# Attention scores of a two-layer block: from bf16 products over 96 rows, one head at a time, to float32r products of two heads in the two row halves of TensorE

## The chip, the cores and the metric

The kernel runs on one core of one Trainium2 chip. The metric is the device time of one execution in microseconds (us), lower is better; it is the median over several executions. The kernel is written straight against the engines: each engine has its own list of instructions, and semaphores order them against each other.

## What is computed

Two transformer layers on a tensor `x` of 2 batches x 512 tokens x 512 features, all in float32. Each layer normalises `x`, and adds an attention branch and a gated feed-forward branch that both read the normalised `x`:

```python
xn = _layernorm(x, axis=-1)
x = x + _L0_attn_ref(xn, ...) + _L0_ffn_ref(xn, ...)
xn = _layernorm(x, axis=-1)
x = x + _L1_attn_ref(xn, ...) + _L1_ffn_ref(xn, ...)
# attention of both layers, H = 32 heads of HD = 16 features, T = 512 tokens
scores = einsum('bhqd,bhkd->bhqk', q, k)            # causal, scaled by 1/sqrt(HD)
weights = softmax(scores, axis=-1)
ctx = einsum('bhqk,bhkd->bhqd', weights, v)         # then @ Wo + bo
# layer 0 shares the keys and values of 8 groups among 32 heads
# feed-forward: down(silu(gate(x)) * up(x)), 1792 hidden features, then 1376
```

## The kernel before

**The dense work.** Every dense product is made of three float32r products: both operands are split into a high part, rounded to float32r, and a low part (`three_passes`, L1245). The weights come in chunks of 128x512 (256 KB) over the SP queue; ACT makes the high part `w_hi` (L988), POOL the low part `w_lo` (L921). A projection step (`proj`) takes one chunk and issues 12 matmuls of 128x512 into a bank of `g_ring` (2 banks); the steps `out` and `v1` issue matmuls of 128x256 into the two `acc` banks, `v0` those of 128x128.

**Attention** is cut into 32 units: 4 phases (layer, batch) x 8 units of four heads each (`4 * QUADS`). A unit has 10 jobs; a job fills one PSUM bank of 512 columns with causal blocks. All four heads of a unit have four query tiles of 128; a tile attends to 128, 256, 384 or 512 keys. For a unit there are these steps:

- `S` (L1358), 10 per unit: the scores with queries as rows. A head has only 16 features; both operands are split into three bf16 parts each, and `Q_PARTS` and `K_PARTS` stack six products of parts, so the contraction is 6 x 16 = 96 rows. DVE adds the causal mask and takes each row's maximum (`smax`, L1213).
- `msplit` on POOL (L943 to L947) splits the negated maxima into three bf16 parts, `Mt` (L1366) transposes them, `mrow` (L1223) copies them out, and two DMAs put them as rows 96 to 98 under the queries of `q_op`; under the keys of `k_op` stand rows of ones.
- `T` (L1381), 10 per unit: the scores again, with keys as rows and 96 + 3 = 99 contraction rows, so that the maximum is already subtracted. ACT takes the exponential of the bank's 512 columns (`exp`, L981), POOL masks the diagonal blocks (`mask`, L968).
- `PV` (L1399), 3 per unit: the masked exponentials times the values and a column of ones, in full float32, four heads side by side in column tiles of 17 (heads at partitions 0, 32, 64, 96 of `pv_ps`). ACT copies the result (`oev`, L994), `otr` (L1408) transposes it, DVE divides by the sums (`norm`).

`S`, `T` and `Mt` share a ring of three PSUM banks (`s_ring`, `wait_ring`). The queries and keys of eight heads (an octet) go from `proj` through `qhi` (ACT, L1030), `qres` (DVE, L1154), `qmid` (ACT, L1035) and `qlo` (POOL, L933) to DRAM and come back with six DMAs each (L866), one per stacked part.

**The order of the work** on each engine is made by `plan()`: a list `fill` of dense steps in fixed order, and queues of attention steps with a due place in it (`S_AT`, `T_AT`, `PV_AT`). It goes by tables of costs (`PE_US`, `ACT_US`, ...). Nearly every attention step thus stands between dense steps.

**The start** has 22 matmuls that only keep PE at work (L1268), then the layer norms of both batches. Of these early tiles the first is normalised on DVE (L1123) and eleven on POOL (L928); each is transposed by PE (L1281) into `g_ring`, from which ACT and DVE make `xt_hi` and `xt_lo`.

## Time and profile before

| what | value |
|---|---|
| median of 3 executions | 942.08 us (941.6 to 943.6) |
| the profiled execution, its time | 943.2 us |
| its span in the profile | 941.6 us |
| PE busy | 887.2 us (94%) |
| DVE, ACT, POOL busy | 524.5, 458.0, 497.5 us |
| DMA | 91.01 MB, mean 97 GB/s |
| mean granted TensorE clock | 0.98 |

PE is TensorE's matmul side, PEld its weight loads, SP the queue that issues all DMAs. Matmuls are pipelined: a row's duration runs from the issue of a matmul to its modelled end and overlaps the next ones. What a matmul costs when the engine is full is therefore the distance between the starts of two following rows, not the duration in them. In a timeline the first number is the start in us, the second the duration in us, and what stands in brackets is the idle time before it and what ended it.

### The profile page before, as it was taken

What the parts mean: (1) busy time and instruction counts of PE and PEld (TensorE: products, weight loads), DVE (VectorE), ACT (ScalarE), POOL (GpSimd) and SP (SyncE); (2) the same over time, 40 slices, a digit from 0 to 9 for tenths busy, and PEclk for the clock granted to TensorE, in tenths of its full rate; (3) what the DMA queues carried; (4) which work ended last, traced back from release to release, by engine and by line L of the source; (5) the groups of instructions that cost most, each with busy time, mean ns of one, the idle gap of its engine ahead of it and who ended that gap; (6) DMA issues with size and microseconds to landing.
All of it is one profiled execution on the core that took longest, in us unless ns stands there. A gap on an engine that the chain in (4) does not pass through costs nothing. (4 is left out here: it accounts for less than half of the span.)

```text
span 941.6 us, 16765 instructions
## 1 busy us (share of the span) xinstructions
PE 887.2 (94%) x5790; PEld 645.2 (69%) x5790; DVE 524.5 (56%) x1543; ACT 458.0 (49%) x838; POOL 497.5 (53%) x747
## 2 busy tenths in 40 slices
PE   6778999999999899999999999999999999999887
PEld 3654655666788666677678886677667876566677
DVE  5455454756756656644576566545476474454353
ACT  2343444545646435444475555444375454344542
POOL 6834445453565534555555665455455666454343
PEclk7889999999999999999999999999999999999999
DMA  6534151523241421527172642827344463721131
GB/s 190 123 106 105 41 119 36 119 68 87 77 89 58 108 68 47 119 84 154 57 145 71 148 95 75 159 67 136 90 113 106 107 140 106 149 63 61 54 90 35
DMA packets 62146, 91.01 MB, mean 97 GB/s; under 512 B 9104, under 2 KB 31120, under 8 KB 62064
## 3 DMA queue, kind: packets, MB, share of 16 engines
q1 hardware_dynamic: 62064, 89.95, 39.6%
q8 instruction: 47, 0.77, 0.3%
q14 instruction: 35, 0.29, 0.1%
HBM read 77.21 MB, written 12.71 MB: 95 GB/s over the span
## 5 line engine op out<-in xcount | busy, mean ns | idle before, releaser
L921 POOL TENSOR_TENSOR w_lo<-w_raw,w_hi 128x512 fp32r<-128x512 f32 x204 | 268.3, 1320 | 84.6 <-ACT w_hi L988 80.8
L981 ACT ACTIVATE p<-s_ring 128x512 f32<-128x512 f32 x320 | 183.4, 597 | 175.2 <-PE s_ring L1381 174.5
L1213 DVE CUSTOM_DVE_ANT_0 s_ring<-s_ring,causal 128x384 f32<-128x384 f32 (+3 forms) x512 | 239.0, 515 | 48.1 <-PE s_ring L1358 47.2
L968 POOL TENSOR_SCALAR_AFFINE_SELECT p<-p 128x256 f32<-128x256 f32 (+1 forms) x320 | 121.0, 381 | 255.2 <-ACT p L981 252.8
L1245 PE MATMUL g_ring<-xt_hi,w_hi 128*128 128x512 f32 (+1 forms) x504 | 214.4, 425 | 6.8 <-DVE xt_lo L1143 3.1
L1245 PE MATMUL g_ring<-xt_lo,w_hi 128*128 128x512 f32 (+1 forms) x504 | 200.2, 397 | 0.0
L1245 PE MATMUL g_ring<-xt_hi,w_lo 128*128 128x512 f32 (+1 forms) x504 | 199.6, 396 | 0.0
L988 ACT ACTIVATE w_hi<-w_raw 128x512 fp32r<-128x512 f32 x204 | 127.6, 627 | 51.0 <-PE acc L1245 25.0
L1381 PE MATMUL s_ring<-q_op,k_op 99*128 99x384 bf16 (+3 forms) x512 | 118.8, 304 | 12.3 <-DVE maxima L1213 6.2
L1245 PE MATMUL acc<-w_hi,h_hi 128*128 128x256 f32 (+1 forms) x400 | 123.3, 308 | 4.1 <-DVE h_lo L1194 4.1
L1358 PE MATMUL s_ring<-k_op,q_op 96*128 96x384 bf16 (+3 forms) x512 | 115.8, 303 | 8.9 <-DVE maxima L1213 4.5
L1245 PEld LDWEIGHTS g_ring<-xt_hi,w_hi 128*128 128x128 f32 (+1 forms) x504 | 96.4, 191 | 35.4 <-DVE xt_lo L1140 3.8
L1245 PE MATMUL acc<-w_lo,h_hi 128*128 128x256 f32 (+1 forms) x400 | 113.7, 284 | 0.0
L1245 PE MATMUL acc<-w_hi,h_lo 128*128 128x256 f32 (+1 forms) x400 | 113.3, 283 | 0.0
L1194 DVE TENSOR_TENSOR h_lo<-h,h_hi 128x512 fp32r<-128x512 f32 (+1 forms) x100 | 90.6, 918 | 38.0 <-ACT h_hi L1041 37.8
L1245 PEld LDWEIGHTS g_ring<-xt_hi,w_lo 128*128 128x128 f32 (+1 forms) x504 | 96.2, 191 | 22.2
L1245 PEld LDWEIGHTS g_ring<-xt_lo,w_hi 128*128 128x128 f32 (+1 forms) x504 | 96.6, 192 | 17.4
L1399 PE MATMUL pv_ps<-p,v_op 128*17 128x512 f32 (+3 forms) x1024 | 88.5, 440 | 0.2 <-POOL p L968 0.2
L1245 PEld LDWEIGHTS acc<-w_hi,h_hi 128*128 128x128 f32 (+1 forms) x400 | 76.8, 192 | 10.3 <-issue 7.4
L1179 DVE SCALAR_TENSOR_TENSOR gate<-gate,g_ring 128x512 f32<-128x512 f32 (+1 forms) x50 | 34.4, 688 | 87.2 <-ACT gate L1000 87.2
L1358 PEld LDWEIGHTS s_ring<-k_op,q_op 96*128 96x128 bf16 x512 | 39.0, 98 | 64.1 <-ACT p L981 21.8
L1381 PEld LDWEIGHTS s_ring<-q_op,k_op 99*128 99x128 bf16 x512 | 37.6, 98 | 63.5 <-DVE maxima L1213 23.0
(86 smaller groups left out, 1138.9 us busy)
## 6 DMA issues: line engine op xcount, KB each, us to landing
w_raw<-weights_in SPq DMA_DIRECT2D x204, 256.0 KB, 2.7
q_op<-qk_scratch SPq DMA_DIRECT2D x96, 128.0 KB, 4.4
qk_scratch<-qk_parts SPq DMA_DIRECT2D x26, 384.0 KB, 2.6
k_op<-qk_scratch SPq DMA_DIRECT2D x48, 128.0 KB, 4.3
x<-x_in SPq DMA_DIRECT2D x8, 256.0 KB, 4.5
y_out<-x SPq DMA_DIRECT2D x8, 256.0 KB, 2.6
k_op<-qk_scratch SPq DMA_DIRECT2D x24, 64.0 KB, 3.0
bo_all<-bo_in SPq DMA_DIRECT2D x2, 256.0 KB, 5.1
```

Of the source, the lines that this page charges most:

```text
L921: pool.tensor_tensor(w_lo[:, c % SPLIT, :], w_raw[:, c % RAW, :], w_hi[:, c % SPLIT, :].bitcast(F32), ALU.subtract).then_inc(split_done, 1)
L968: pool.affine_select(out=view, in_=view, compare_op=ALU.is_ge, fill=0.0, base=0, pattern=[[0, n], [1, P]] if n == 2 else [[1, P]], channel ...
L981: act.activation(p32[:, j % PRING, :], s_ring[r % SRING][:, :], ACT.Exp, scale=SCALE).then_inc(exp_done, 1)
L988: act.activation(w_hi[:, c % SPLIT, :], w_raw[:, c % RAW, :], ACT.Copy).then_inc(whi_done, 1)
L1179: dve.scalar_tensor_tensor(out=gate[0:m, n % 2, :], in0=gate[0:m, n % 2, :], scalar=1.0, in1=g_ring[g % 2][0:m, :], op0=ALU.add, op1=ALU.m ...
L1194: dve.tensor_tensor(h_lo[0:rows, hs % HSPLIT, :], h[0:rows, f, :], h_hi[0:rows, hs % HSPLIT, :].bitcast(F32), ALU.subtract).then_inc(hlo_d ...
L1213: last = dve.tensor_tensor_reduce(out=s_ring[r % SRING][:, at:at + n], in0=s_ring[r % SRING][:, at:at + n], in1=causal[:, 512 - n:], scale ...
L1245: ins = pe.matmul(dst, w[a], xa[c], start=first and i == 0, stop=last and i == 2, skip_group_check=skip)
L1358: last = pe.matmul(s_ring[r % SRING][:, at:at + n], q_op[0:QROWS, u // 2 % 2, 4 * (u % 2) + j, qt * P:(qt + 1) * P], k_op[0:QROWS, ks, kh, ...
L1381: last = pe.matmul(s_ring[r % SRING][:, at:at + n], k_op[0:MROWS, ks, kh, kt * P:(kt + 1) * P], q_op[0:MROWS, u // 2 % 2, 4 * (u % 2) + j, ...
L1399: last = pe.matmul(pv_ps[32 * j:32 * j + VW, kt * P:T], v_op[:, slot, kt, vh, :], p32[:, (JOBS * u + job) % PRING, at:at + T - kt * P], st ...
```

## The change

- The operands of the scores are no longer bf16 but float32r, in high and low parts: a query stands as (high, low, high), a key as (high, high, low), so a product has 3 x 16 = 48 rows, and `T` has 50, since the maximum is now two rows. The steps `qmid`, `qlo` and `msplit` are gone; `Mt` transposes the float32 maxima, and `mrow` makes both parts in two DVE instructions.
- Even heads stand on partitions 0 to 49, odd heads on 64 to 113 of `q_op` and `k_op` (`ROW_TILE = 64`, `operands`). Two jobs, one of an even and one of an odd head, are issued block by block in turn, each into its own bank.
- A PE step `ST` (a visit) issues two jobs of `S` and two of `T`, the latter 7 visits behind. There are 5 visits per unit, 167 in all (the first 7 have only `S`, the last 7 only `T`). `S` has two banks `s_bank`, `T` two in one tensor `t_banks`. Before it a visit waits for the maxima of the visit before, and ahead of its `T` part for the exponential of the visit before.
- ACT takes one exponential of 128x1024 over both `t_banks` (L1004), 160 in place of 320.
- `PV` is one step of all 16 products per unit instead of three, and takes a bank of `g_ring`; `pv_ps` is gone.
- The queries and keys go to DRAM already stacked (three DMAs of 256 KB) and come back with two DMAs of 48 partitions; layer 0's keys are read again for every octet (`kin`).
- At the start all early tiles are normalised on DVE, four at a time, and transposed into the four score banks; 28 and 8 matmuls keep PE at work in place of 22, and the second octet's queries are projected in the start.
- The planner's constants and the places of the steps are set anew.

```diff
-MROWS = QROWS + 3
-Q_PARTS = (0, 0, 1, 0, 1, 2)
-K_PARTS = (0, 1, 0, 2, 1, 0)
+QROWS = 3 * HD
...
+def score_blocks(job):
+
+    if job < 4:
+        return ((job, 3, 0),)
+    if job < 8:
+        return ((job - 4, 0, 3 * P), (job - 4, 2, 0))
+    return ((job - 8, 1, 0), (job - 6, 1, 2 * P))
+
+
...
+RAW, SPLIT, HSPLIT, PRING, EARLY_BANKS = 4, 4, 3, 14, 4
+VISITS = JOBS // 2
+LAG = VISITS + 2
+SCORE_VISITS = 4 * QUADS * VISITS
...
+        def begin():
+            if kind == "x":
+                ln_stats(0, b)
+            else:
+                ln_rms(b)
+            for tt in range(TT):
+                end["xn", first + tt] = place("dve", at("stats", 0, b, kind), "xn", 0, b, kind, tt,
+                                              ("early", first + tt), first + tt)
...
+    def filler(i, count):
+        return [(0.0, lambda: 0.0, lambda: line["pe"].append((state["t"], len(line["pe"]), ("busy", i, count))))]
+
+    q1 = w_octet(0, 1, 0)
+    prologue = (ln_0 + filler(0, 8) + ln_1[:1] + q + k0 + ln_1[1:3] + w_v(0, 0, 0) + ln_1[3:] + k1 + w_v(0, 1, 1) + ln_n[:3] + q1
+                + ln_n[3:] + rms_1)
     ffn00 = w_ffn(0, 1)
...
-        q_op = sb("q_op", [MROWS, 2, 8, T], BF16)
-        k_op = sb("k_op", [MROWS, 2, 8, T], BF16)
+        q_op = sb("q_op", [P, 2, 4, T], F32R)
+        k_op = sb("k_op", [P, 2, 4, T], F32R)
...
-        s_ring = [ctx.enter_context(nc.psum_tensor(f"s_ring{i}", [P, 512], F32)) for i in range(SRING)]
+        s_bank = [ctx.enter_context(nc.psum_tensor(f"s_bank{i}", [P, 512], F32)) for i in range(2)]
+        t_banks = ctx.enter_context(nc.psum_tensor("t_banks", [P, 2, 512], F32))
+        t_bank = [t_banks[:, i, :] for i in range(2)]
...
+        def operands(u, j):
+
+            rows = ROW_TILE * (j % 2)
+            slot, pair = u // 2 % 2, 2 * (u % 2) + j // 2
+            k_pair = u % 2 if u < 2 * QUADS else pair
+            return rows, slot, pair, k_pair
...
                 elif kind == "qkin":
                     _, n, what, l, b, octet = s
...
+                    dst, here = (q_op, q_here) if what == "q" else (k_op, k_here)
+                    if octet >= 2:
+                        sp.wait_ge(t_made, t_count(2 * octet - 3))
+                    for half in range(2):
+                        rows = ROW_TILE * half
+                        sp.dma_start(dst[rows:rows + QROWS, octet % 2, :, :].bitcast(F32),
+                                     qk_scratch[n % 2].rearrange("r (p two) t -> two r p t", two=2)[half]
+                                     ).then_inc(here[octet % 2], 16)
...
-                elif kind == "xn":
...
-                    pool.tensor_scalar(h[:, own, :], x[:, b * TT + tt, :], mv[:, b, tt, 0:1],
-                                       scale[:, b, tt:tt + 1], ALU.subtract, ALU.mult).then_inc(xn_pool_done, 1)
-                elif kind == "qlo":
...
-                elif kind == "msplit":
...
                 if kind == "exp":
-                    _, r, j, i = s
-                    act.wait_ge(ring_made, n_ring[r])
+                    _, j, u, i = s
+                    act.wait_ge(t_made, t_count(u, i))
                     if j >= PRING:
-                        act.wait_ge(pv_done, n_pv[pv_of_job(j - PRING)])
-                    act.activation(p32[:, j % PRING, :], s_ring[r % SRING][:, :], ACT.Exp, scale=SCALE
+                        act.wait_ge(pv_done, 4 * n_pv[(j + 1 - PRING) // JOBS])
+                    act.activation(p32[:, j % PRING:j % PRING + 2, :], t_banks[:, :, :], ACT.Exp, scale=SCALE
                                    ).then_inc(exp_done, 1)
...
                 elif kind == "smax":
-                    _, r, u, i = s
-                    dve.wait_ge(ring_made, n_ring[r])
-                    if i == 0 and u == 0:
+                    _, u, job = s
...
+                    bank = s_bank[job % 2]
+                    for j, qt, at in score_blocks(job):
                         n = (qt + 1) * P
+                        column = 8 * (j % 2) + 4 * (j // 2) + qt
...
-                elif kind == "S":
-                    _, r, u, i = s
-                    wait_ring(r)
...
-                    for j, qt, at in score_blocks(i):
-                        n = (qt + 1) * P
-                        ks, kh = k_slot_and_head(u, j)
-                        last = pe.matmul(s_ring[r % SRING][:, at:at + n],
-                                         q_op[0:QROWS, u // 2 % 2, 4 * (u % 2) + j, qt * P:(qt + 1) * P],
-                                         k_op[0:QROWS, ks, kh, 0:n], start=True, stop=True)
-                    last.then_inc(ring_made, 1)
+                elif kind == "ST":
+                    v = s[1]
+                    if v < SCORE_VISITS:
+                        u, i = divmod(v, VISITS)
+                        if i:
+                            pe.wait_ge(smax_done, max(n_smax[(u, 2 * i - 2)], n_smax[(u, 2 * i - 1)]))
+                        elif u:
+                            pe.wait_ge(smax_done, n_smax[(u - 1,)])
+                        else:
+                            pe.wait_ge(g_freed, max(last_early[0], last_early[1]))
+                        if i == 0:
+                            octet = u // 2
+                            pe.wait_ge(q_here[octet % 2], arrival[("q", octet)])
+                            pe.wait_ge(k_here[octet % 2], arrival[("k", octet)])
+                        blocks = [score_blocks(job) for job in (2 * i, 2 * i + 1)]
+                        for n_block, pair in enumerate(zip(*blocks)):
+                            for j, qt, at in pair:
+                                n = (qt + 1) * P
+                                r, slot, p, kp = operands(u, j)
+                                ins = pe.matmul(s_bank[j % 2][:, at:at + n],
+                                                q_op[r:r + QROWS, slot, p, qt * P:(qt + 1) * P],
+                                                k_op[r:r + QROWS, slot, kp, 0:n], start=True, stop=True)
+                                if n_block == len(blocks[0]) - 1:
+                                    ins.then_inc(s_made, 1)
+                    if v >= LAG:
+                        t_u, i = divmod(v - LAG, VISITS)
+                        if v > LAG:
+                            pe.wait_ge(exp_done, n_exp[JOBS * t_u + 2 * i - 2])
+                        else:
+                            pe.wait_ge(g_freed, max(last_early[2], last_early[3]))
+                            pe.wait_ge(rows_here, 64)
+                        if i == 0:
+                            pe.wait_ge(m_here[t_u % 2], 32 * (t_u // 2 + 1))
+                        blocks = [trans_blocks(job) for job in (2 * i, 2 * i + 1)]
+                        for n_block, pair in enumerate(zip(*blocks)):
+                            for j, kt, at in pair:
+                                n = T - kt * P
+                                r, slot, p, kp = operands(t_u, j)
+                                ins = pe.matmul(t_bank[j % 2][:, at:at + n],
+                                                k_op[r:r + MROWS, slot, kp, kt * P:(kt + 1) * P],
+                                                q_op[r:r + MROWS, slot, p, kt * P:T], start=True, stop=True)
+                                if n_block == len(blocks[0]) - 1:
+                                    ins.then_inc(t_made, 1)
                 elif kind == "Mt":
-                    _, r, u = s
-                    wait_ring(r)
-                    pe.wait_ge(msplit_done, n_msplit[u])
-                    pe.transpose(s_ring[r % SRING][:, :].bitcast(BF16)[0:48, 0:P],
-                                 m_parts[:, u % 2, :, :].rearrange("p s g -> p (s g)"), ident16[:, :]
-                                 ).then_inc(ring_made, 1)
...
                 elif kind == "PV":
-                    _, u, n_step = s
+                    _, g, u = s
                     l, b = PHASES[u // QUADS]
-                    if n_step == 0:
-                        if u == 0:
-                            pe.wait_ge(ones_made, 1)
-                        if u % QUADS == 0:
-                            pe.wait_ge(acc_freed, max(v_made[(0, 0)], v_made[(0, 1)]) if l == 0 else v_made[(1, b)])
-                        if u:
-                            pe.wait_ge(oev_done, n_oev[u - 1])
-                    pe.wait_ge(mask_done, n_mask[JOBS * u + LAST_JOB[n_step]])
-                    for j, kt, job, at in PV_BLOCKS[n_step]:
+                    wait_g(g)
+                    if u == 0:
+                        pe.wait_ge(ones_made, 1)
+                    if u % QUADS == 0:
+                        pe.wait_ge(acc_freed, max(v_made[(0, 0)], v_made[(0, 1)]) if l == 0 else v_made[(1, b)])
+                    pe.wait_ge(mask_done, max(n_mask[JOBS * u + job] for job in range(JOBS)))
+                    for j, kt, job, at in PV_BLOCKS:
                         slot, vh = v_head(u, j)
-                        last = pe.matmul(pv_ps[32 * j:32 * j + VW, kt * P:T], v_op[:, slot, kt, vh, :],
-                                         p32[:, (JOBS * u + job) % PRING, at:at + T - kt * P],
-                                         start=kt == 0, stop=kt == 2, skip_group_check=True)
-                    last.then_inc(pv_done, 1)
+                        ins = pe.matmul(g_ring[g % 2][32 * j:32 * j + VW, kt * P:T], v_op[:, slot, kt, vh, :],
+                                        p32[:, (JOBS * u + job) % PRING, at:at + T - kt * P],
+                                        start=kt == 0, stop=kt == 2, skip_group_check=True)
+                        if kt == 2:
+                            ins.then_inc(pv_done, 1)
```

How the instructions move on PE, in the gate and up projections of the third phase (numbers stand for buffers; `k_op,q_op` are `S`, `q_op,k_op` are `T`). Before, jobs of one bank stand alone or in pairs, and the product with the values comes in three places:

```order
L1358 MATMUL s_ring2<-k_op,q_op 128x384
L1358 MATMUL s_ring2<-k_op,q_op 128x128
L1381 MATMUL s_ring0<-q_op,k_op 128x384
L1381 MATMUL s_ring0<-q_op,k_op 128x128
L1399 MATMUL pv_ps<-p32,v_op 17x512 x4
L1358 MATMUL s_ring1<-k_op,q_op 128x256 x2
L1245 MATMUL g_ring0<-xt_hi,w_hi 128x512
```

The changed kernel has, at about the same place of PE's list, one step of values and then a whole visit:

```order
L1422 MATMUL g_ring0<-p32,v_op 17x512 x4
L1422 MATMUL g_ring0<-p32,v_op 17x384 x4
L1422 MATMUL g_ring0<-p32,v_op 17x128 x4
L1422 MATMUL g_ring0<-p32,v_op 17x256 x4
L1383 MATMUL s_bank0<-k_op,q_op 128x128
L1383 MATMUL s_bank1<-k_op,q_op 128x128
L1383 MATMUL s_bank0<-k_op,q_op 128x384
L1383 MATMUL s_bank1<-k_op,q_op 128x384
L1402 MATMUL t_banks<-q_op,k_op 128x512 x2
L1260 MATMUL acc0<-w_hi,h_hi 128x256
```

The jobs are bundled by four, and blocks of the two row halves alternate.

On POOL, the start before (L928 normalises a tile, L921 makes `w_lo`, L933 the third part of a query or key):

```order
L928 TENSOR_SCALAR h<-x,mv,rstd 128x512 x3
L921 TENSOR_TENSOR w_lo<-w_raw,w_hi 128x512 x4
L928 TENSOR_SCALAR h<-x,mv,rstd 128x512
L933 TENSOR_TENSOR qk_parts<-rest,qk_parts 128x512
L928 TENSOR_SCALAR h<-x,mv,rstd 128x512 x2
L933 TENSOR_TENSOR qk_parts<-rest,qk_parts 128x512
L928 TENSOR_SCALAR h<-x,mv,rstd 128x512
```

And now, where L969 makes `w_lo`:

```order
L963 MEMSET p 2x2048
L969 TENSOR_TENSOR w_lo<-w_raw,w_hi 128x512 x16
L991 AFFINE_SELECT p<-p 128x128 x2
```

The chunks' low parts stand at the head of POOL's list, and the tiles of the layer norm are DVE's (`L1134 TENSOR_SCALAR`, four in a row ahead of the four `xt_lo`).

## Rows read from the trace of the kernel before

**Rows 1.** The page: span, and the busy time of each engine.
```profile
span 941.6 us, 16765 instructions
PE 887.2 (94%) x5790; PEld 645.2 (69%) x5790; DVE 524.5 (56%) x1543; ACT 458.0 (49%) x838; POOL 497.5 (53%) x747
```
**Rows 2.** Busy time by stretch; the last three columns are PEclk, DMA share, GB/s.
```profile
core 0: us, PE busy (x) PEld busy (x) DVE busy (x) ACT busy (x) POOL busy (x), PEclk, DMA share, GB/s
0.00:24.00 24.00, 15.71 (x53) 9.24 (x54) 13.38 (x36) 6.42 (x12) 14.80 (x18) 0.79 0.62 186
24.00:100.00 76.00, 63.25 (x347) 45.00 (x345) 41.24 (x132) 29.36 (x62) 41.18 (x47) 0.89 0.45 105
100.00:880.00 780.00, 757.11 (x4982) 543.03 (x4984) 443.38 (x1343) 397.52 (x725) 418.02 (x662) 1.00 0.41 96
```
**Rows 3.** The page's costliest groups: both score products, the exponential.
```profile
L981 ACT ACTIVATE p<-s_ring 128x512 f32<-128x512 f32 x320 | 183.4, 597 | 175.2 <-PE s_ring L1381 174.5
L1381 PE MATMUL s_ring<-q_op,k_op 99*128 99x384 bf16 (+3 forms) x512 | 118.8, 304 | 12.3 <-DVE maxima L1213 6.2
L1358 PE MATMUL s_ring<-k_op,q_op 96*128 96x384 bf16 (+3 forms) x512 | 115.8, 303 | 8.9 <-DVE maxima L1213 4.5
```
**Rows 4.** Timeline of PE alone, around 300 us: full-size float32r and bf16 matmuls.
```profile
300.27 0.40 PE L1245 MATMUL g_ring<-xt_lo,w_hi 128*128 128x512 f32 x1
300.51 0.39 PE L1245 MATMUL g_ring<-xt_hi,w_lo 128*128 128x512 f32 x1
...
305.98 0.39 PE L1358 MATMUL s_ring<-k_op,q_op 96*128 96x512 bf16 x1
306.21 0.38 PE L1381 MATMUL s_ring<-q_op,k_op 99*128 99x512 bf16 x1
306.43 0.60 PE L1408 MATMUL g_ring<-ident,o_t 128*128 128x128 f32 x4
```
**Rows 5.** Timeline of PE: a 256-column step of values, what follows, and float32r restarting.
```profile
303.33 0.63 PE L1399 MATMUL pv_ps<-p,v_op 128*17 128x256 f32 x8
303.89 0.39 PE L1381 MATMUL s_ring<-q_op,k_op 99*128 99x512 bf16 x1
304.11 0.60 PE L1281 MATMUL g_ring<-ident,xn 128*128 128x128 f32 x4
304.47 0.36 PE L1245 MATMUL acc<-w_hi,h_hi 128*128 128x256 f32 x1
304.67 0.28 PE L1245 MATMUL acc<-w_lo,h_hi 128*128 128x256 f32 x1
304.79 0.28 PE L1245 MATMUL acc<-w_hi,h_lo 128*128 128x256 f32 x1
```
**Rows 6.** Timeline of PE: a 512-column step of values between its neighbours.
```profile
813.11 0.40 PE L1245 MATMUL g_ring<-xt_lo,w_hi 128*128 128x512 f32 x1
813.34 0.40 PE L1245 MATMUL g_ring<-xt_hi,w_lo 128*128 128x512 f32 x1
813.67 1.05 PE L1399 MATMUL pv_ps<-p,v_op 128*17 128x512 f32 x8
814.65 0.39 PE L1358 MATMUL s_ring<-k_op,q_op 96*128 96x256 bf16 x2
```
**Rows 7.** The chain of waits: a step of values with 384 and 128 columns.
```profile
844.52 0.99 PE pv_ps L1399 x16
```
**Rows 8.** Timeline of PE: float32r matmuls of 128 columns.
```profile
26.45 0.27 PE L1245 MATMUL acc<-w_hi,xt_lo 128*128 128x128 f32 x1
26.57 0.27 PE L1245 MATMUL acc<-w_hi,xt_hi 128*128 128x128 f32 x1
```
**Rows 9.** Timeline of POOL, the start; first tiles of the layer norm.
```profile
9.13 6.47 POOL L928 TENSOR_SCALAR h<-x,mv,rstd 128x512 f32<-128x512 f32 x3 [6.12 <-DVE rstd L1070]
15.56 5.01 POOL L921 TENSOR_TENSOR w_lo<-w_raw,w_hi 128x512 fp32r<-128x512 f32 x4
```
**Rows 10.** Timeline of all engines, the start: the first projection, a tile on DVE, `xt_lo`.
```profile
9.05 0.55 DVE L1123 TENSOR_SCALAR h<-x,mv,rstd 128x512 f32<-128x512 f32 x1
...
17.49 0.69 DVE L1140 TENSOR_TENSOR xt_lo<-g_ring,xt_hi 128x512 fp32r<-128x512 f32 x1 [1.36 <-ACT xt_hi L1017]
...
18.33 0.76 PE L1245 MATMUL g_ring<-xt_hi,w_hi 128*128 128x512 f32 x1 [1.50 <-DVE xt_lo L1140]
```
**Rows 11.** Timeline of PE, 36 to 53 us: two of six waits, 8.8 us together.
```profile
36.90 0.89 PE L1281 MATMUL g_ring<-ident,h 128*128 128x128 f32 x4 [2.55 <-POOL h L928]
...
52.62 0.66 PE L1281 MATMUL g_ring<-ident,h 128*128 128x128 f32 x4 [1.96 <-DVE xt_lo L1143]
```
**Rows 12.** Groups by shape: the maxima of a full bank, and reading each out.
```profile
L1213 DVE CUSTOM_DVE_ANT_0 s_ring<-s_ring,causal 128x512 f32<-128x512 f32 x128 | 86.7, 705 | 23.7 <-PE s_ring L1358 23.6
...
L1213 DVE DVE_READ_ACCUMULATOR2_ANT maxima<- 128x1 f32 x512 | 72.0, 141 | 0.0
```

532 lines of the change are left out of this document (247 added, 285 removed).

## The prediction

> **What bounds the kernel now.** I read the page first: PE is busy for 887.2 of 941.6 us, no other engine for more than 56% [rows 1]. The stretches then say where PE is not full [rows 2]: from 100 to 880 us it is busy for 757.1 of 780 us at the full clock, 2.4 GHz; in the first 24 us for 15.7, in the next 76 for 63.3, at a mean granted clock of 0.79 and 0.89 of full. So there are two problems: a long middle in which only less PE work shortens the run, and a start in which PE waits. The third view, the groups of the score products, shows how small their waits are: 12.3 and 8.9 us before 1024 matmuls [rows 3]. The last views are timelines of PE, read for the distance between starts, because durations overlap.
>
> **Prices from the timelines.** A float32r matmul of 512 columns takes 0.23 us from start to start (I take 0.228, since two distances of the timeline show 0.24 and 0.22), a bf16 one of 512 columns 0.23 and 0.22 [rows 4]: the type makes no difference at this size. Float32r at 256 columns is 0.12 [rows 5], at 128 columns 0.12 or 0.11 [rows 8], of which I take 0.11; for 384 columns I take 0.17, between 256 and 512. A step of values with 512 columns takes 0.98 us from its start to the next, and the start itself comes 0.10 later than the neighbour's 0.23 [rows 6]; one with 256 columns takes 0.56 [rows 5]; one with 384 and 128 takes 0.99 [rows 7]. So 256 columns more cost 0.42 us, and what does not depend on columns is 0.56 - 0.42 = 0.14 plus 0.10 = **0.24 us for one entry into column tiles and back**. The eight records of such a step, four heads, run side by side: 1.05 us holds them all.
>
> **The change, part by part.**
>
> *Scores, before.* 640 jobs of 512 columns each (some two blocks) at 0.225 us are 144 us.
>
> *Scores, after.* The columns are the same, but blocks of an even and an odd head are issued in turn on different row halves and write different banks. No trace of before shows row halves. The bounds: both heads run side by side, as four heads do in column tiles [rows 6], or one after the other as all else does [rows 4]. I take side by side, as the nearest row is also a tiling. A unit then has for `S` two pairs of each size, 2 x (0.228 + 0.17 + 0.12 + 0.11) = 1.26 us, for both `S` and `T` 2.51, in 32 units 80 us. To this comes the fixed cost of a visit. Nearest is the 0.24 of the column tiles; its weights have only 17 columns, those of a visit 128 in float32, and where float32r begins anew after another kind the first distance is 0.20 and not 0.12 [rows 5], so 0.08 more. 167 visits x 0.32 = 53 us. Sum 134 us, **10 us less** than 144. The bounds of the fixed part are zero (row halves need no entry) and 0.24 + 0.20 with both first loads in the open: 0 to 73 us.
>
> *Values.* Before, 0.98 + 0.99 + 0.56 + 3 x 0.10 = 2.83 us a unit. As one step, 1280 columns x 0.42/256 + 0.24 = 2.34. 32 x 0.49 = **16 us less**. The step now takes a bank of `g_ring` until ACT has copied it; the other bank covers that with a projection of 12 x 0.228 = 2.7 us. Where a short transpose follows instead, PE waits about a half microsecond; this I leave in the range.
>
> *Waits at the scores.* The 21.2 us [rows 3] belong to a ring of three banks and 640 steps. Now there are 167 steps with two waits each, on average 942/167 = 5.6 us apart; what they wait for is the maxima of two jobs, 2 x (0.705 + 0.141) = 1.7 us of DVE [rows 12], and one exponential of 1024 columns, at most two of 0.597 [rows 3]. Both fit into the 5.6 us, so I take **5 us less**, not more, since a wait now holds four jobs and all dense work behind it in PE's order.
>
> *The start.* POOL's three tiles take 6.47 us, and its first `w_lo` can begin only at 15.56 [rows 9]; a tile takes DVE 0.55 us [rows 10]. Now DVE makes four tiles from 9.05 to 11.3 and then four `xt_lo` at 0.69 [rows 10], to 14.1, while POOL makes `w_lo` from the start. The first projection can begin at about 14.3 instead of 18.33 [rows 10]: 4 us. Later in the start six waits of PE for POOL's tiles and `xt_lo`, where two banks hand over to each other, sum to 8.8 us [rows 11]; with four banks and no POOL I take 6 of them, and 2 us of the time that PE runs at the half clock, 1.2 GHz (0.89 over 76 us is 17 us at half, 8 us lost [rows 2]). **12 us less.** The bounds are 4 and 20.
>
> *At nothing.* `qmid`, `qlo` and `msplit` leave ACT and POOL, which are busy for 49 and 53% [rows 1]. `mrow` gets a second instruction on DVE, two visits ahead of its use. The queries' and keys' traffic grows by some 12 MB on 91; the DMA share is 0.41 in the middle [rows 2]. These hide behind dense PE work; if a load came late, PE would stop at the first visit of one of 16 octets.
>
> **Sum.** 10 + 16 + 5 + 12 = 43 us. The profiled execution took 943.2 us, 1.1 more than the median, so the sum is 900.2 against it, and against the median of 942.08 it is 899; I say 900.
>
> **A rule against this.** The timeline shows weight loads of full-array float32r hidden: matmuls of 256 columns stand 0.12 us apart although each loads 128 columns [rows 5]. *The Trainium skill (TensorE: Matmul & The Clock Gate, Part 3) says that a weight load overlaps matmuls in flight only where its row group differs; here all row groups are the same, and the trace disagrees with it.* If it held inside a row half, 16 pairs per unit would each show one load of 0.08, of which 5 are counted: 11 x 0.08 x 32 = 28 us more, 928 us. *The Trainium skill (TensorE: Matmul & The Clock Gate, Part 3) also gives 3.07x for four row tiles in place of 4x; by that factor, an estimate, the 80 us of columns would be 104 and the time 924.*
>
> **Rivals.**
> - *The two heads' loads go one after the other.* Then no pair is faster than two loads, 2 x 0.11 = 0.22, whatever its columns. A unit has 16 pairs: 4 x 0.228 + 12 x 0.22 = 3.55 instead of 2.51, 33 us more: **933**. For it: a 128-column float32r matmul is no faster than 0.11, though a quarter of the columns of 512 would be 0.06 [rows 4, 8], so a load seems to set the pace there. Against it: four loads and four matmuls of a step of values go together.
> - *Unhidden loads inside a row half*, 928, above. Against it rows 5.
> - *Row halves give no overlap*, so the change doesn't do what it says. The columns cost 5.02 a unit, 161 us instead of 80: **981**, slower.
> - *The visit's waits take over*: this is the one on the other side that I hold likeliest. A visit waits for DVE and for ACT, and PE's order lets no dense step pass it. It decides from 43/167 = 0.26 us of wait per visit more than I took; DVE and ACT are each busy for half the time with other steps of 0.6 to 0.7 us, so one such step ahead of the maxima or of the exponential is enough where visits stand close. At 0.4 us per visit, 67 us: **967**. Against it: two jobs of maxima and a dense step of 2.7 us between visits.
> - *Faster than I say*: row halves need no entry, and a visit costs only the 0.08: 40 us less, **860**.
>
> **How the numbers follow.** My forecast has 0.63, loads in turn 0.12, unhidden loads 0.05, no overlap 0.05, waits 0.08, no entry cost 0.07. The likeliest gives 900 us, with 880 to 920 as its own range from the bounds of the start (8 us either way) and of the fixed part. The range must take in the rivals at 928 and 933 and part of the faster one: 870 to 940. A measurement of this kernel can tell about 0.2%, 2 us, from no change. Faster: 0.63 + 0.12 + 0.05 + 0.07, less a little for what I haven't seen: 0.85. Same 0.02, slower 0.13.
>
> **What would show it.** In the profile of the changed kernel: score matmuls of one pair start within some hundredths of a microsecond of each other, and pairs of 512 columns stand 0.23 apart; pairs of 128 columns 0.11 (0.22 if loads go in turn); a visit of 512-column pairs spans some 0.75 us from its start to that of the next dense step; a step of values 2.3 to 2.4; the first projection near 14 us; less than 20 us of PE waits before score matmuls. I am wrong in the main if the pairs of a head follow each other at 0.23, or if PE's idle time between 100 and 880 us grows beyond its present 23 us.

## The result: slower, 962.1 us against 942.8

| | before | after |
|---|---|---|
| median, measured together | 942.84 us (941.6 to 944.75) | 962.08 us (960.72 to 973.48) |
| ratio, 95% interval | | 1.0234 (1.0165 to 1.0303) |
| the profiled execution, its time | 943.2 us | 973.48 us |
| its span | 941.6 us | 971.3 us |

I had forecast 900, and a range of 870 to 940. A fifth execution of after, of 967.04 us, is on record and counts in the ratio; the two medians alone stand at 1.020. The profiled execution of after is 11 us above its median, so its rows overstate the loss somewhat; where a size matters I use medians of runs.

Page of after: the span, the busy time, the granted clock in 40 slices, and the shares of the chain that ended last, by engine and by line.

```profile
span 971.3 us, 16201 instructions
PE 879.4 (91%) x5804; PEld 670.4 (69%) x5804; DVE 530.2 (55%) x1584; ACT 440.9 (45%) x652; POOL 400.5 (41%) x551
...
PEclk9989999976999999998989989989998989999999
...
PE 60%; DMA 23%; DVE 6%; SPq 4%; ACT 3%; issue 3%; POOL 1%; POOLq 0%; ACTq 0%; DVEq 0%
PE g_ring L1260 28%; PE acc L1260 16%; DMA qk_scratch<-qk_parts 11%; DMA k_op<-qk_scratch 6%; PE s_bank L1383 5%; PE g_ring L1422 5%; DMA w_raw<-weights_in 4%; PE t_banks L1402 3%; SPq L889 2%; SPq L900 1%; DVE s_bank L1224 1%; PE g_ring L1432 1%; DMA q_op<-qk_scratch 1%; ACT p L1004 1%; DVE qk_parts L1163 1%
```

PE is busy for 8 us less in a run that is 30 us longer [rows 1]. 23% of the chain is now DMA, and the trips of queries and keys out (`qk_scratch<-qk_parts`, 11%) and back (6% and 1%) are 18%. POOL lost 97 us of work; outside the start PE had waited for it less than 2 us.

The same stretches as in [rows 2], of after; the last columns are PEclk, DMA share, GB/s.

```profile
0.00:24.00 24.00, 20.40 (x94) 12.32 (x95) 18.11 (x44) 8.19 (x16) 9.13 (x16) 1.00 0.56 190
24.00:100.00 76.00, 65.03 (x345) 50.56 (x345) 43.19 (x135) 27.66 (x54) 25.26 (x28) 0.93 0.52 135
100.00:880.00 780.00, 712.20 (x4756) 540.00 (x4756) 431.46 (x1331) 364.06 (x522) 327.70 (x463) 0.95 0.40 106
```

At the start PE is busier and its clock higher (14 of its matmuls are additional ones of the kind that only keeps it at work: 36 in place of 22). The middle is where it went: PE idle for 67.8 us instead of 23, and the clock down to 0.95. What PE waits for there, from the view of waits of after (us in total, times, longest), and the group of the first score product:

```profile
PE s_bank L1383 <- DMA k_op<-qk_scratch: 33.4, 8, 6.7
PE g_ring L1432 <- ACT o_t L1017: 12.6, 12, 6.2
PE s_bank L1383 <- DMA k_op<-k_scratch: 8.6, 1, 8.6
...
PE s_bank L1383 <- DVE m_rows L1236: 4.2, 5, 1.2
PE s_bank L1383 <- DVE maxima L1224: 4.0, 7, 0.9
...
L1383 PE MATMUL s_bank<-k_op,q_op 48*128 48x128 f32 (+3 forms) x512 | 87.6, 400 | 51.4 <-DMA k_op<-qk_scratch 33.4
```

Where [rows 3] had 8.9 us, now 51.4. Eight times the first visit of an octet stands and waits for its keys: these are the eight octets of layer 1, whose keys have just been projected and make the whole trip. The 8.6 us are the very first visit, at 52 us, which waits for layer 0's keys in the start. The maxima, which I had thought about most, are 4.0 us.

How one such wait comes about: the chain of after at 480 us (start, duration, what), and SyncE's own list for the same time.

```profile
480.50 6.24 DMA qk_scratch<-qk_parts
...
490.03 9.54 DMA qk_scratch<-qk_parts
...
500.21 7.05 DMA k_op<-qk_scratch
...
507.40 0.80 PE s_bank L1383 x2
```
```profile
479.18 1.95 SPq L889 DMA_DIRECT2D qk_scratch<-qk_parts  x3
...
486.75 1.24 SPq L900 DMA_DIRECT2D q_op<-qk_scratch  x2
488.04 0.59 SPq L854 DMA_DIRECT2D w_raw<-weights_in  x1
488.72 2.64 SPq L889 DMA_DIRECT2D qk_scratch<-qk_parts  x3
499.59 1.23 SPq L900 DMA_DIRECT2D k_op<-qk_scratch  x2
```

The queries go out, SyncE waits until they are in DRAM (L900 needs that), reads them back, fetches one chunk of weights, and only then sends the keys out: 9.5 us, and 7.0 back. From the first issue to the score visit it is 28 us. PE's last dense matmul started at 500.4, the visit at 507.4. The planner had priced the same trips at 2 and 4 us (`TRANSFER`, the table of steps). The list of DMA issues has the sizes (KB each, median us to landing); before, 384 KB out took 2.6 us and 128 KB back 4.3 to 4.4.

```profile
w_raw<-weights_in SPq DMA_DIRECT2D x204, 256.0 KB, 2.9
qk_scratch<-qk_parts SPq DMA_DIRECT2D x72, 256.0 KB
q_op<-qk_scratch SPq DMA_DIRECT2D x32, 384.0 KB, 6.2
k_op<-qk_scratch SPq DMA_DIRECT2D x16, 384.0 KB, 6.5
```

A projection's parts are now float32 words, and three of them are written out: 768 KB instead of 384.

The second wait, for `o_t`, has in its longest case the same origin. Chain of after at 210 us:

```profile
210.68 7.98 DMA w_raw<-weights_in
...
218.68 0.02 ACT w_hi L1011
...
219.22 0.59 ACT o_t L1017
...
219.94 1.09 PE g_ring L1432 x4
```

Weights were issued behind a load of queries and keys and took 8.0 us instead of 2.9, the median. ACT works in its order, so `w_hi` held up `o_t`, and `o_t` held up PE.

The visits themselves came out as forecast. Timeline of PE of after: a visit and a step of values, each with what follows it.

```profile
306.03 0.28 PE L1260 MATMUL acc<-w_hi,h_lo 128*128 128x256 f32 x1
306.24 0.49 PE L1383 MATMUL s_bank<-k_op,q_op 48*128 48x512 f32 x2
306.57 0.45 PE L1402 MATMUL t_banks<-q_op,k_op 50*128 50x128 f32 x4
306.95 0.39 PE L1260 MATMUL acc<-w_hi,h_hi 128*128 128x256 f32 x1
...
314.35 2.35 PE L1422 MATMUL g_ring<-p,v_op 128*17 128x512 f32 x32
316.63 0.39 PE L1260 MATMUL acc<-w_hi,h_hi 128*128 128x256 f32 x1
```

A visit with 1024 columns of `S` and as many of `T` takes 0.71 us to the next dense matmul (forecast 0.75), entered 0.09 later than the dense pitch of 0.12. The two matmuls of a pair start 0.003 us apart in the trace's records: two heads in row halves do run side by side. The step of values takes 2.28 us (forecast 2.34).

### The profile page after: what moved, and what is told of

It is laid out like the page before. It is cut to its first block, busy times and chain, and to the rows that moved or that the text cites. A ratio compares the mean times of both kernels' runs of the same rounds, so it can differ in the third digit from the quotient of the medians.

```text
span 971.3 us, 16201 instructions
## 1 busy us (share of the span) xinstructions
PE 879.4 (91%) x5804; PEld 670.4 (69%) x5804; DVE 530.2 (55%) x1584; ACT 440.9 (45%) x652; POOL 400.5 (41%) x551
## 4 chain that ended last, share of the span: by engine, by line
PE 60%; DMA 23%; DVE 6%; SPq 4%; ACT 3%; issue 3%; POOL 1%; POOLq 0%; ACTq 0%; DVEq 0%
PE g_ring L1260 28%; PE acc L1260 16%; DMA qk_scratch<-qk_parts 11%; DMA k_op<-qk_scratch 6%; PE s_bank L1383 5%; PE g_ring L1422 5%; DMA w_raw<-weights_in 4%; PE t_banks L1402 3%; SPq L889 2%; SPq L900 1%; DVE s_bank L1224 1%; PE g_ring L1432 1%; DMA q_op<-qk_scratch 1%; ACT p L1004 1%; DVE qk_parts L1163 1%
## 5 line engine op out<-in xcount | busy, mean ns | idle before, releaser
L969 POOL TENSOR_TENSOR w_lo<-w_raw,w_hi 128x512 fp32r<-128x512 f32 x204 | 263.4, 1292 | 225.1 <-ACT w_hi L1011 224.9
L1224 DVE CUSTOM_DVE_ANT_0 s_bank<-s_bank,causal 128x128 f32<-128x128 f32 (+3 forms) x512 | 236.7, 519 | 110.0 <-PE s_bank L1383 109.5
L1004 ACT ACTIVATE p<-t_banks 128x1024 f32<-128x1024 f32 x160 | 164.1, 1025 | 53.7 <-PE t_banks L1402 48.6
L1383 PE MATMUL s_bank<-k_op,q_op 48*128 48x128 f32 (+3 forms) x512 | 87.6, 400 | 51.4 <-DMA k_op<-qk_scratch 33.4
L1260 PE MATMUL acc<-w_hi,h_lo 128*128 128x256 f32 (+1 forms) x400 | 119.3, 298 | 0.0
L1383 PEld LDWEIGHTS s_bank<-k_op,q_op 48*128 48x128 f32 x512 | 42.5, 191 | 98.8 <-issue 81.9
L1203 DVE TENSOR_TENSOR h_lo<-h,h_hi 128x512 fp32r<-128x512 f32 (+1 forms) x100 | 80.5, 815 | 48.1 <-ACT h_hi L1060 47.4
L1260 PEld LDWEIGHTS acc<-w_hi,h_hi 128*128 128x128 f32 (+1 forms) x400 | 83.0, 208 | 12.3 <-issue 10.4
L1060 ACT ACTIVATE h_hi<-h 128x512 fp32r<-128x512 f32 (+1 forms) x100 | 61.9, 629 | 55.3 <-PE acc L1260 51.6
L1260 PEld LDWEIGHTS acc<-w_lo,h_hi 128*128 128x128 f32 (+1 forms) x400 | 83.5, 209 | 0.0
L1260 PEld LDWEIGHTS acc<-w_hi,h_lo 128*128 128x128 f32 (+1 forms) x400 | 83.1, 208 | 0.0
```

The source lines that it names most:

```text
L969: pool.tensor_tensor(w_lo[:, c % SPLIT, :], w_raw[:, c % RAW, :], w_hi[:, c % SPLIT, :].bitcast(F32), ALU.subtract).then_inc(split_done, 1)
L1004: act.activation(p32[:, j % PRING:j % PRING + 2, :], t_banks[:, :, :], ACT.Exp, scale=SCALE).then_inc(exp_done, 1)
L1060: act.activation(h_hi[0:rows, hs % HSPLIT, :], h[0:rows, f, :], ACT.Copy).then_inc(hhi_done, 1)
L1203: dve.tensor_tensor(h_lo[0:rows, hs % HSPLIT, :], h[0:rows, f, :], h_hi[0:rows, hs % HSPLIT, :].bitcast(F32), ALU.subtract).then_inc(hlo_d ...
L1224: last = dve.tensor_tensor_reduce(out=bank[:, at:at + n], in0=bank[:, at:at + n], in1=causal[:, 512 - n:], scale=1.0, scalar=LOWEST, op0=A ...
L1260: ins = pe.matmul(dst, w[a], xa[c], start=first and i == 0, stop=last and i == 2, skip_group_check=skip)
```

## The experiments

Two theories. **Loads:** the change does on the engines what I computed, and loses it because queries and keys arrive after the visit that wants them; the loss is set by the length of the round trip against the distance in PE's order between projection and visit. **Engines:** the visits, with their four jobs and two waits, or the clock, cost the time, and the waits for DMA only stand where something else would. In the first texts on record the former is theory A; each of the later texts says what its own A and B are.

### 1. Both kernels without the loads

In after, the trips of octets 2 to 15 are left out; the scores of these octets use the operands of the first two, so the result is other data. Semaphore counts follow.

```diff
+                elif kind in ("qkin", "kin") and s[-1] >= 2 or kind == "qkout" and s[1] >= 4:
+                    continue
...
-            k_pair = u % 2 if u < 2 * QUADS else pair
+            k_pair = u % 2
```

> The changed kernel without the traffic of the queries and keys of octets 2 to 15 (neither to DRAM nor back; the scores of those octets use what octets 0 and 1 left, so this part of the result is other data). Theory A, late loads: the 42 us of PE waits for these loads vanish, and with them the half clock that follows each; 890 to 908 us, mean granted clock 0.98 or more. Theory B, the visits themselves (row halves) cost the time or let the clock fall: only the waits go, 920 to 930 us, clock still below 0.97.

The same in before:

```diff
+                elif kind in ("qkout", "qkin") and s[1] >= 4:
+                    continue
```

> The kernel before with the same traffic left out (octets 2 to 15). PE waits for these loads only 1.9 us in its trace: both theories expect 936 to 941 us. The difference to the changed kernel without loads is what the change is worth in the engines alone: 30 to 45 us by theory A, 10 to 20 by theory B.

Measured: after without loads **903.46 us** (902.25 to 905.53; ratio 0.9584, 0.9567 to 0.96), before without loads 939.97 (ratio 0.9967, 0.9953 to 0.9982). So the loads of these octets cost before 3 us and after 962.1 - 903.5 = 59 us, and everything else in the change is worth 940.0 - 903.5 = **36.5 us**; my forecast of that part was 43. The stretch of 100 to 880 us of after without loads:

```profile
100.00:880.00 780.00, 750.31 (x5230) 569.26 (x5223) 462.01 (x1395) 399.46 (x573) 361.13 (x503) 0.99 0.22 65
```

The visits still wait for maxima there, 6.5 us in all. The theory of the engines is out as the main cause. The 36.5 us still contain one late load, since the trips of the first two octets were left in:

```profile
PE s_bank L1386 <- DMA k_op<-k_scratch: 7.9, 1, 7.9
```

Before has no wait for keys above 0.8 us, so the engines' part alone is somewhat more than 36.5.

The two traces, of after with and without loads, also tell what the loads do to PE. Its 5804 matmuls are the same in the same order, so the distances from start to start can be compared one by one; together they differ by 69.6 us (more than the medians do, since the profiled execution of after is the longest of its five). 42.6 us lie in 22 distances that differ by more than 0.45 us, which are the waits. 28.6 us lie in distances that ran at half the granted clock with the loads and at full clock without them, 3.2 in the opposite case, and 1.6 us are left. At each of the eight waits for layer 1's keys stands a stretch at half clock, 51 us together, where the run without loads has none. So the late loads cost PE the waits, 43 us, and the clock around them, 25 us.

### 2. Telling the planner how long a trip takes

```diff
-        end["qkout", n] = place("sp", max(lo, reuse), "qkout", n, kind, l, b) + TRANSFER
+        end["qkout", n] = place("sp", max(lo, reuse), "qkout", n, kind, l, b) + 4 * TRANSFER
...
-                                                      l, b, octet) + 2 * TRANSFER
+                                                      l, b, octet) + 3.5 * TRANSFER
...
-            end["k", octet] = ... "kin", octet) + 2 * TRANSFER
+            end["k", octet] = ... "kin", octet) + 3.5 * TRANSFER
```

> The changed kernel, with only the planner's constants for these loads set to what the trace shows (8 us out in place of 2, 7 us in in place of 4), so that dense work is put where PE waited, as far as there is any that fits. Theory A: the waits for loads fall from 42 us to below 20, 930 to 945 us. Theory B: less than 10 us gained, above 950.

Measured 926.91 us (924.47 to 928.72; ratio 0.9828, 0.9808 to 0.9849). No instruction is added or removed; the planner only puts dense steps where PE stood. 35 us for three constants. The waits for `k_op` are 12.5 us in six places.

### 3. Projecting earlier

```diff
-                due[ph][4 * o + QK_AT] = due[ph].get(4 * o + QK_AT, []) + w_octet(...)
+                early = max(4 * o - 2, 0)
+                due[ph][early] = due[ph].get(early, []) + w_octet(...)
```

> The changed kernel with the projections of an octet's queries and keys due one unit (two half-unit slots) earlier, except those pinned at a phase's first slot; nothing else. Theory A: most waits for loads go, some 8 to 10 us of them stay at the octets that did not move, 915 to 930 us. Theory B: above 945 us.

Measured 924.36 us (923.47 to 925.49; ratio 0.9804, 0.9789 to 0.9818). The bytes are as in after; only the distance grew, and the waits for `k_op<-qk_scratch` fell from 33.4 to 2.9 us.

### 4. A shorter trip

The high part is written once and read twice: 512 KB out instead of 768, four loads back instead of two. Layer 0's keys still go out in three parts.

```diff
-                    for at in range(3):
+                    for at in range(3 if what == "k" and l == 0 else 2):
...
+                        sp.dma_start(dst[rows + pair:rows + pair + 2 * HD, octet % 2, :, :].bitcast(F32),
+                                     from_dram[0:2 * HD]).then_inc(here[octet % 2], 16)
+                        sp.dma_start(dst[rows + single:rows + single + HD, octet % 2, :, :].bitcast(F32),
+                                     from_dram[0:HD]).then_inc(here[octet % 2], 16)
```

> The changed kernel, but a query's or (layer 1) key's high part goes to DRAM once and is read twice: 512 KB out instead of 768, four loads in instead of two, the same bytes in. If the loads are late because too many bytes go out, the way out (6.2 and 9.5 us in the trace) shortens by a third and the run by 10 to 20 us, 942 to 952. If it is the number of transfers and their queueing that counts, no gain or a loss: 958 to 966.

Measured 927.47 us (925.98 to 927.66; ratio 0.9837, 0.9808 to 0.9865), far below the 942 to 952 that I expected. Here PE's order is that of after, matmul by matmul; only the trip is shorter. In the two traces the waits shrink by 25.6 us, and 20.0 more come back in distances that no longer run at half clock. SyncE's wait until a projection is out, behind which weights stand too, fell from 90.7 us to 68.1. So each end of the balance alone, the length of the trip or the distance, gives back some 35 of the 59 us. I had expected such a cure to be additive and small. But a trip that is 4 us late on average (33.4/8) has to become only that much shorter or start that much earlier, and each cure alone does most of this.

### 5. Matmuls that keep the clock

Half the loss, I thought, was the clock that falls while PE waits. Sixteen bf16 matmuls of 512 columns before the waiting visit in seven octets, that change no value:

```diff
+                        if i == 0 and u in (18, 20, 22, 24, 26, 28, 30):
+                            for _ in range(16):
+                                pe.matmul(s_bank[0][:, :], ident16[:, :], causal[:, :], start=True, stop=True)
```

> The changed kernel with 16 dummy bf16 matmuls of 512 columns (3.5 us at the full clock) into the free bank s_bank0 ahead of the wait for the loads of octets 9 to 15. The waits for loads stay. If half of the loss is the clock that falls in these waits, the half-clock time goes from 104 us to below 75 and the run to 942 to 952 us. If the clock costs nothing beyond the wait, 960 to 966.

Measured: three executions of 951.84, 958.86 and 964.78 us (ratio 1.0169, 1.0099 to 1.0239); a fourth, of 2875 us, is left out of the ratio, and its cause I don't know. Waits of the profiled execution:

```profile
PE s_bank L1386 <- DMA k_op<-qk_scratch: 12.6, 6, 4.1
PE g_ring L1435 <- ACT o_t L1017: 11.7, 12, 4.9
```

21 us less of waiting, for 7 x 16 x 0.225 = 25 us of added matmuls. By its clock records PE spent 69.7 us at half clock, against 104.5 in after. Put beside the trace of after, so that a distance before a visit holds its wait and the added matmuls together, the distances that ran at half clock give back 10.7 us, the rest takes 1.9 more, and the two spans differ by 8.8. But the executions of after differ as much among themselves: spans of 971.3, 964.9, 960.8, 959.0 and 958.6 us, at mean granted clocks of 0.947, 0.957, 0.960, 0.962 and 0.964. The interval overlaps that of after (1.0165 to 1.0303), so no gain in time is shown. The clock has its price here, but filling the wait with empty work isn't shown to be a remedy.

### 6. Two parts of the change alone, in before

*One step of values in place of three*, in its own bank as before (`LAST_JOB = (9,)`, all of `PV_BLOCKS` in one tuple):

> The kernel before with the three steps of values of a unit made one (all 16 products in one place, the bank pv_ps as before), and nothing else of the change. By the price of 0.24 us for an entry into column tiles, two entries less per unit: 927 to 932 us. A rival: the later product holds back the ring of exponentials and nothing is gained, 938 to 945.

Measured **950.87 us** (948.67 to 953.92; ratio 1.009, 1.0057 to 1.0124): slower by 7 us. The steps of values did shrink: counted from the start of each to the start of what follows, 77.2 us instead of 84.7. But the other steps moved too. Waits of this kernel (in before, maxima at L1381 6.2, `k_op` 1.9 us):

```profile
PE s_ring L1381 <- DVE maxima L1213: 7.8, 16, 1.0
PE s_ring L1358 <- DMA k_op<-qk_scratch: 7.5, 4, 5.0
...
PE s_ring L1358 <- ACT p L981: 4.0, 11, 1.1
```

The scores' own time, counted in the same way, rose from 168.5 to 178.6 us, and half clock from 39.4 to 62.8 us. 5.6 us of the new waiting are once more for keys, and behind the longest of these waits, 5.0 us at 715 us, stand 10.2 us at half clock. So this run doesn't tell what the merged step costs by itself: the moved order made loads late too, and how much of the 7 us is theirs is open. What the merged step brings in company with the pairs of banks is seen only in the sum of 36.5.

*All early tiles normalised on DVE*, still with two banks:

```diff
-            engine = "dve" if own == 0 else "pool"
-            xn = place(engine, at("stats", l, b, kind), "xn", l, b, kind, tt, g, own)
+            xn = place("dve", at("stats", l, b, kind), "xn", l, b, kind, tt, g, own)
```

> The kernel before with the early tiles of the layer norm all on DVE instead of POOL, still through two banks of g_ring. Of the 12 us that I gave to the new start this should bring 5 to 9: 933 to 938 us, first projection at 15 to 16 us instead of 18.3. A rival: the hand-over of two banks sets the pace, below 3 us.

Measured 941.42 us (938.7 to 944.06; ratio 0.9979, 0.996 to 0.9997), 2 to 3 us faster. By the traces' records the 97th dense matmul starts at 45.6 us before, at 40.7 here and at 35.1 after; the 145th at 61.5, 56.8 and 53.2. So in the start the tiles on DVE bring about half of the gain. The other half came with the rest of the new start, four banks among it, which no run takes apart; and by the end of this run only 2 to 3 us of the gain are left.

### 7. Doubling only the bytes out, in before

```diff
                     sp.dma_start(qk_scratch[n % 2], qk_parts[:, n % 2, :, :]).then_inc(qk_out[n % 2], 16)
+                    sp.dma_start(qk_again[n % 2], qk_parts[:, n % 2, :, :]).then_inc(qk_out[n % 2], 16)
```

> The kernel before, which writes its 384 KB per projection out of the chip twice, the second time into a DRAM tensor of its own (no value changes): the bytes written of the change, without anything else of it. Theory A (the change lost by a longer round trip against a distance that also became shorter): out takes 5 us or more instead of 2.6, the kernel before has less slack than that at some octets, 948 to 958 us. Theory B (bytes alone are harmless as long as the plan's distance is that of before): 942 to 947 us.

Measured **959.98 us** (958.37 to 961.62; ratio 1.0172, 1.0149 to 1.0194): 16 us slower, with nothing else of the change. Its issues and its largest wait:

```profile
qk_scratch<-qk_parts SPq DMA_DIRECT2D x26, 384.0 KB, 2.3
qk_again<-qk_parts SPq DMA_DIRECT2D x26, 384.0 KB, 3.2
...
PE s_ring L1360 <- DMA k_op<-qk_scratch: 12.2, 5, 3.5
```

The wait was 1.9 us before. The median landing barely changed; what grew is SyncE's wait until the parts are out, from 56.7 to 74.8 us at the same place. Before, the balance stood without slack, and 10 MB more on 91 were enough to tip it. This is the term that I put at nothing, measured by itself in the kernel before.

### 8. The cures together

Two parts out, two slots earlier, and the planner at 2.5 and 3 x `TRANSFER`:

> The change with three cures together: two parts out of the chip instead of three (512 KB), the projections planned two slots earlier, and the planner told of transfers of 5 us out and 6 us in. Theory A (what the change lost is the round trip of queries and keys finishing after the score visit that wants it, and each cure alone took a part of the same wait): PE waits for k_op of at most 3 us from 100 us on, 906 to 918 us. Theory B (a good part of the remaining 21 to 24 us over the run without loads is what the transfers cost even when early, by queuing ahead of the weights, so that the wait behind o_t and the weight loads stays): 919 to 926 us, with the waits for o_t at 8 us or more.

Measured **913.92 us** (911.75 to 914.61; ratio 0.968, 0.9659 to 0.9701), 30 us faster than before and 48 faster than after. Its largest waits:

```profile
PE s_bank L1393 <- DVE m_rows L1246: 9.3, 10, 1.2
PE g_ring L1442 <- ACT o_t L1027: 8.3, 8, 6.0
PE s_bank L1393 <- DVE maxima L1234: 5.1, 9, 0.7
```

No wait for `k_op` is left among them. Above the run without loads it lies by 10 us. The waits for `o_t` (8.3 against 3.1) and for the rows of maxima (9.3 against 4.2) are 10 us longer; but the run without loads has 7.9 us of waiting for its first keys, which this one has not, so the account doesn't close.

With the first octets of a phase also projected in the phase before:

```diff
+                early = (ph, max(4 * o - 2, 0)) if o or ph == 0 else (ph - 1, 14)
```

> As the run with the three cures, and the first octet after each start of a phase is projected one phase earlier too (slot 14 of the phase before), so that no octet from the fifth on is projected less than 40 us of TensorE work ahead. Theory A: 1 to 6 us below the run with the three cures, 902 to 914 us, no wait for k_op<-qk_scratch above 1 us in all. Theory B: within 2 us of the run with the three cures, since the waits left are for the weights and at the start.

Measured 935.24 us (934.2 to 936.95; ratio 0.9916, 0.9892 to 0.994), 21 us slower than the run above, where both theories had it equal or better. No wait for `k_op` stands among its twelve largest; the largest is for `o_t`, 19.6 us, and the chain shows the worst one:

```profile
255.38 8.40 DMA w_raw<-weights_in
...
263.81 0.02 ACT w_hi L1022
...
264.35 0.59 ACT o_t L1028
```

Within 5.7 us SyncE had issued 512 KB out of one projection, 768 KB back of the one before and 384 KB of keys, all ahead of these weights; ACT stood 11.4 us at `w_hi`. Of 16 us that PE stands longer between 100 and 880 us than in the run above, 11 are for `o_t`. Earlier is better only until the trips meet each other.

If weights behind trips are the trouble, let the weights go first:

```diff
+    for i in range(len(SP)):
+        j = i
+        while SP[j][0] == "wload" and j and SP[j - 1][0] in ("qkin", "kin") and SP[j - 1][-1] >= 2:
+            SP[j - 1], SP[j] = SP[j], SP[j - 1]
+            j -= 1
```

> The run with the three cures, in which each load of queries or keys of the third octet and later stands in SyncE's queue behind the loads of weights that follow it at once, instead of ahead of them. Theory A (the stall of 6.3 us at 209 us, PE behind o_t behind w_hi behind weights that are queued behind the query and key loads, is a matter of that queue's order): the wait for o_t falls from 8.3 to below 3 us and the time by 3 to 8 us, 906 to 911 us. Theory B (the loads of queries and keys then finish later and the wait only changes its name, since SyncE now holds them back until the weights' buffers are free): k_op or q_op waits of 5 us or more come back, 912 to 922 us.

Measured 970.83 us (964.73 to 972.91; ratio 1.0298, 1.0271 to 1.0325), the slowest of all. Waits of PE and of SyncE:

```profile
PE s_bank L1398 <- DMA k_op<-qk_scratch: 40.1, 6, 10.9
...
PE g_ring L1447 <- ACT o_t L1032: 2.2, 6, 0.9
...
SPq L865 <- POOL w_lo L984: 380.3, 115, 9.7
```

The wait for `o_t` fell as the first theory says, from 8.3 to 2.2 us. But a weight load on SyncE waits until POOL has freed a buffer (296.0 us of waiting in the run above, 380.3 here), and now the keys stood behind that. Theory B was right in kind, but it had 912 to 922 us; neither had the size.

## Why the prediction was wrong

By its own steps:

- **"At nothing": the traffic. This step failed.** "These hide behind dense PE work" did not hold: the trip of queries and keys ended after the visit that wanted them. The text named the place ("if a load came late, PE would stop at the first visit of one of 16 octets") and set neither a price nor a rival beside it. What the rows of before would have given: 384 KB out in 2.6 us and six loads that land 4.3 us after their issue, by the list of DMA issues; twice the bytes out, so 5 or more; SyncE, which does nothing else while it waits for the parts (56.7 us in 24 waits before, by the view of SyncE's waits), issues queries and keys in turn. The planner's constants stayed at 2 and 4 us while its PE work between projection and visit shrank with every microsecond that the change saves. A DMA share of 0.41 says nothing on this: it is a mean, and the trip is a chain. Measured: 59 us for the loads of octets 2 to 15 in after against 3 in before; 16 us in before for doubled bytes out alone; 35 us back by the planner's constants alone. What the runs do not part is bytes from order: none sent the keys out ahead of the queries' way back, or over another queue.
- **Scores, 10 us less, and waits, 5 less.** Better than forecast. Counted from the start of each run of score matmuls to the start of what follows, 168.5 us before and 126.8 in after without loads; 167 entries at 0.10 us lie outside this count, so 25 us less where I had 15 (the wait ahead of a run is outside the count in both). The price of a visit was right: 0.71 and 0.09 of entry for a visit with pairs of 512, 128 and 384 columns, where columns and fixed part made 0.228 + 0.11 + 0.17 + 0.32 = 0.83. So the undersized part is what the ring of three banks cost between its steps before; this is what is left over, and no run shows it alone.
- **Values, 16 us less.** In size right: 2.28 us a step, and 84.7 us before against 73.8 after without loads by the same count, with 64 entries at 0.10 outside it, so 17. As a change by itself in before it brought 7 us more, late keys among them.
- **The start, 12 us less.** 8 to 10 us by the place of the same dense matmul, and the first visit's wait of 8.6 us for its keys, which the term did not have, lies between the two places at 35.1 and 53.2 us. The first projection started at 16.52 us, not 14.3, behind the four `xt_lo` of DVE, since DVE's first tile began at 11.97 and not at 9.05: two instructions on 4 columns ahead of it took 1.26 and 1.18 us, where before (L1069, L1070) they took 0.17 and 0.16. They last as long as POOL makes its first two `w_lo`, which before stood behind POOL's tiles. In the run with only the tiles moved to DVE it is the same, 1.25 and 1.18 us beside `w_lo` from 8.75 to 11.24, and there too the first projection comes late, at 17.24. The clock of the first 24 us is 1.00.

```profile
9.42 2.50 POOL L969 TENSOR_TENSOR w_lo<-w_raw,w_hi 128x512 fp32r<-128x512 f32 x2 [4.64 <-ACT w_hi L1011]
9.45 1.26 DVE L1088 TENSOR_SCALAR newton<-newton 128x4 f32<-128x4 f32 x1
10.75 1.18 DVE L1089 TENSOR_TENSOR rstd<-rstd,newton 128x4 f32<-128x4 f32 x1
```

- **The terms together.** The spans of the two profiled executions without loads, 940.8 us of before and 901.7 of after, differ by 39.1. Counted from start to start, scores have 41.5 us less, values 10.9 less and all other matmuls of PE 13.3 more, in which the visits' entries stand. So the 903.5 us, near my 900, are partly luck: more than forecast at the scores, about the forecast at the values, and less in all else.
- **The rule against this** (weight loads inside a row half unhidden, 928 us) and **loads in turn** (933) did not come: with either, the two later pairs of the visit at 306.24 would have taken 0.16 us more together, some 0.87; it took 0.71, and its pair of 128 columns is followed by the next pair after 0.06 us, where loads in turn would have made it 0.22. *So the trace of after, too, disagrees with the sentence of the Trainium skill (TensorE: Matmul & The Clock Gate, Part 3) that only another row group lets a weight load overlap.*
- **No overlap** (981) and **the visit's waits** (967) did not come either; that 962 stands near the latter is chance. The wait at the visit is for DMA, not for DVE or ACT.
- **What would show it** was right: "wrong in the main if PE's idle time between 100 and 880 us grows beyond its present 23 us". It grew to 67.8.

The two profiled executions, after against after without loads, differ by 971.3 - 901.7 = 69.6 us. By the view of waits, those for keys and for `o_t` hold 33.4 + 0.7 + 9.5 = 44 of them. The other 26 are the clock, 104.5 us at half clock against 27.7: the comparison distance by distance in experiment 1 gives it 25. The prediction had no term for this either, since it had no wait. The medians differ by 59 and not by 69.6, since the profiled execution of after was its longest, and the one with the lowest granted clock.

## What to carry to other kernels

Where an edit makes data wider that leaves the chip and comes back, follow one trip from its first issue to its user, with every wait of the queue between, and hold it against the distance in the consumer's order, which shrinks by what the edit saves. Price a late load at its wait and at the clock that falls with it, here 25 us beside 43. If a planner sets the order, its transfer constants are part of the edit. And a queue in order has two sides: loads that are moved forward push back others, so look at who stands behind them before you move them.

## Not expected of the hardware

- Two float32r products with 48 or 50 rows each in the two row halves run side by side with their own weight loads of 128 columns: 1024 columns of `S` take 0.33 us and the whole visit 0.71, where 512 columns of one product take 0.23 [rows 4].
- The same weight load of 256 KB lands in 2.9 us by the median and in 8.0 or 8.4 us when it is issued right behind a trip: 768 KB of queries and 384 KB of keys in both places, and 512 KB out besides in the second.
- 768 KB from the chip to DRAM took, from the last of the three issues, 6.2 us in one place and 9.5 us ten microseconds later, against 2.6 for 384 KB, the median of before. In the second place 768 KB of queries on their way back and 256 KB of weights had been issued in the 3.3 us before.
- Two DVE instructions on 128x4, of 0.17 and 0.16 us before, take 1.26 and 1.18 us beside two `w_lo` of POOL (TENSOR_TENSOR on 128x512, 2.50 us) and end with them. When POOL's pair starts at 10.28 us instead of 9.42, in the run of the three cures, they move with it: 1.26 and 1.18 us from 10.31.
- A wait costs more than itself: of the 69.6 us between the traces of after with and without loads, 43 are waits and 25 are matmuls that ran at the half clock instead of the full one.
